# One transformer kernel, the windowed-attention stage: dense products of the gated layer, value projections and key norms assigned to other slots

## The reference, cut to what matters

```python
def _layer(x, wqkv, qs, ksc, wo, lg, lb, w1, b1, w2, b2):
    h = shift_token(x)                      # half of the features come from the token before
    q, k, v = split(h @ wqkv)               # 8 heads of 64
    q = l2norm(q) * qs; k = l2norm(k) * ksc
    q, k = rotary_xpos(q, k)
    o = local_attention(q, k, v)            # windows of 64 keys, each query sees its window and the one before
    x = x + o @ wo
    h = layernorm(shift_token(x)) * lg + lb
    a, g = split(h @ w1 + b1)               # 2 x 341, padded to 2 x 384 in the kernel
    h = a * gelu(g)
    return x + h @ w2 + b2
```

## Time and profile before

| | |
|---|---|
| median of three runs | 4851.66 us |
| the profiled execution, and its span | 4860.0 us, 4858.2 us |
| PE busy / DVE / ACT / POOL over the span | 88% / 61% / 51% / 23% |
| mean granted clock of TensorE | 0.89 |
| pass 0, first to last maximum (777.54 to 1308.02 us) | 530.48 us, granted clock 0.81 |
| pass 1, first to last maximum (1838.14 to 2348.88 us) | 510.74 us, granted clock 0.86 |

### The profile page before, as it was taken

The page is one execution under the profiler, slowest core; times in us unless marked ns, Lnnn a source line. Parts: engine busy times, 40 slices in busy tenths (PEclk is TensorE's granted clock), DMA queues, the critical chain, the costliest instruction groups (busy, mean ns, idle before and its releaser), DMA issues.

```text
span 4858.2 us, 64573 instructions
## 1 busy us (share of the span) xinstructions
PE 4266.8 (88%) x24264; PEld 2057.4 (42%) x24264; DVE 2964.9 (61%) x6559; ACT 2473.9 (51%) x4237; POOL 1116.2 (23%) x1582
## 2 busy tenths in 40 slices
PE   8888878999998889999886777999988999879999
PEld 5212335656532235555553234555553334333343
DVE  4888456656478866666345994666666653466632
ACT  3588634445348774545345553454443663236642
POOL 1100113333210013333112662111121004420024
PEclk8799977788779997988797998999996999979999
DMA  1100102111010011111000000000001000000000
GB/s 49 27 15 13 45 0 70 32 32 37 8 52 21 14 44 38 34 32 30 5 7 5 0 0 16 8 16 8 16 32 26 22 8 0 29 21 21 15 1 9
DMA packets 48024, 104.19 MB, mean 21 GB/s; under 512 B 15064, under 2 KB 15064, under 8 KB 46432
## 3 DMA queue, kind: packets, MB, share of 16 engines
q1 hardware_dynamic: 47712, 100.06, 7.6%
HBM read 40.24 MB, written 1.05 MB: 8 GB/s over the span
## 4 chain that ended last, share of the span: by engine, by line
PE 57%; DVE 17%; ACT 7%; POOL 2%; issue 2%; SPq 1%; DMA 0%; POOLq 0%; DVEq 0%; ACTq 0%
PE PS L446 29%; PE PS L1034 6%; PE PS L981 5%; DVE SM L1108 4%; DVE AR L2355 3%; PE PS L2553 2%; PE PS L1013 2%; ACT AR L453 2%; DVE AR L450 2%; PE PS L1672 1%; PE PS L1717 1%; PE PS L1662 1%; PE PS L473 1%; ACT PS L2298 1%; PE PS L986 1%
## 5 line engine op out<-in xcount | busy, mean ns | idle before, releaser
L1108 DVE TENSOR_REDUCE SM<-PS 128x1 f32<-128x512 f32 (+3 forms) x1792 | 1029.0, 627 | 256.4 <-PE PS L981 161.0
L446 PE MATMUL PS<-AR,WS 128*128 128x512 f32 (+1 forms) x2112 | 1065.8, 644 | 71.9 <-DVE AR L450 32.7
L1082 ACT ACTIVATE AR<-PS 128x1024 f32<-128x1024 f32 (+3 forms) x896 | 825.5, 933 | 338.5 <-PE PS L1016 169.2
L453 ACT ACTIVATE AR<-PS 128x512 f32<-128x512 f32 (+6 forms) x760 | 450.2, 599 | 550.2 <-PE PS L446 415.0
L981 PE MATMUL PS<-AR 51*128 51x512 bf16 (+3 forms) x1792 | 526.7, 390 | 160.9 <-DVE SM L1108 98.9
L446 PEld LDWEIGHTS PS<-AR,WS 128*128 128x128 f32 (+1 forms) x2112 | 404.0, 203 | 529.8 <-issue 406.2
L1740 ACT ACTIVATE AR<-PS,SM 128x128 f32<-128x128 f32 x512 | 229.6, 452 | 472.8 <-DVE SM L1803 470.6
L1034 PE MATMUL PS<-AR 128*32 128x512 f32 (+3 forms) x3584 | 448.6, 573 | 1.3 <-ACT AR L1082 0.9
L981 PEld LDWEIGHTS PS<-AR 51*128 51x128 bf16 x1792 | 129.9, 94 | 678.5 <-DVE SM L1108 477.0
L1013 PE MATMUL PS<-AR 51*128 51x512 bf16 (+3 forms) x1792 | 386.3, 366 | 11.8 <-ACT AR L1082 11.0
L1141 POOL CAST MBT<-SM 128x8 bf16<-128x8 f32 x128 | 28.0, 219 | 1274.3 <-DVE SM L1112 1053.9
(11 more groups left out here) (314 smaller groups left out, 7285.2 us busy)
## 6 DMA issues: line engine op xcount, KB each, us to landing
TP<-RAW SPq DMA_DIRECT2D x512, 64.0 KB, 2.0
AR<-AR SPq DMA_DIRECT2D x768, 32.0 KB
WS<-wall SPq DMA_DIRECT2D x4, 3654.5 KB, 11.1
WS<-wall SPq DMA_DIRECT2D x8, 902.5 KB, 4.6
WS<-wall SPq DMA_DIRECT2D x2, 3334.5 KB, 10.9
WS<-wall SPq DMA_DIRECT2D x1, 2384.0 KB, 9.1
WS<-wall SPq DMA_DIRECT2D x1, 1543.5 KB, 6.2
AR<-pad SPq DMA_DIRECT2D x88, 12.0 KB
```

Source lines behind the costliest of these rows:

```text
L446: t = e.matmul(o, l, r, start=(n == 0), stop=(n == len(pairs) - 1))
L453: return e.activation(o, i, ACT.Copy, scale=1.0)
L1082: e.activation(pv[:, :, off:512], sv[:, :, off:512], ACT.Exp, scale=scale).then_inc(*F.at_exp.up((s, u, p2)))
L1108: e.tensor_reduce(mh[:, at, k0 // 512:k0 // 512 + 1], bank(ring(n + g), m), AX.X, ALU.max, negate=True).then_inc(*F.at_max.up((s, k, i, rr ...
```

## The change

The products of the gated layer of chunk q leave slot 16 q + 39 (n = 7) for three slots, one `gate` and one `up` in each of n = 7, 8 and 11, for q = 0 to 5; `down` goes from n = 8 to n = 13. Norm 3 goes from n = 4 to n = 5, with it the steps of its root from n = 5, 6, 7 to n = 6, 7, 8; v1 goes from n = 11 to n = 12 (in groups with g > 0). What runs behind the units (q = 6, 7) keeps its slots. The number of arithmetic instructions stays; the number of DMAs too.

```diff
-        def gate_slot(q):
-            return 16 * q + 39 if q < 6 else (133, 138)[q - 6]
+        def gate_slots(q):
+            return [16 * q + n for n in (39, 40, 43)] if q < 6 else [(133, 138)[q - 6]] * 3
 
         def down_slot(q):
-            return gate_slot(q) + (2 if q == 6 else 1)
+            return 16 * q + 45 if q < 6 else (135, 139)[q - 6]
...
-                second = [("norm", g, j) for j, at in enumerate((2, 3, 4, 4, 6, 7, 10, 11)) if n == at] + second
+                second = [("norm", g, j) for j, at in enumerate((2, 3, 4, 5, 6, 7, 10, 11)) if n == at] + second
...
-                second += [("v", g, j) for j, at in enumerate((8, 11, 14, 15) if g else (8, 11, 12, 12)) if n == at]
+                second += [("v", g, j) for j, at in enumerate((8, 12, 14, 15) if g else (8, 11, 12, 12)) if n == at]
...
-                if slot_ == gate_slot(q):
+                if q >= 6 and slot_ == gate_slots(q)[0]:
                     first += [("gate", q, 0), ("up", q, 0), ("gate", q, 1)]
                     second += [("up", q, 1), ("gate", q, 2), ("up", q, 2)]
+                if q < 6 and slot_ in gate_slots(q):
+                    first += [("gate", q, gate_slots(q).index(slot_))]
+                    second += [("up", q, gate_slots(q).index(slot_))]
...
-                if g < 8 and n in (5, 6, 7):
+                if g < 8 and n in (6, 7, 8):
                     next(roots[g, 1], None)
```

## The result

The changed kernel takes 4914.48 us (median of four runs, 4905.77 to 4921.73), the one before 4849.32 beside it on the same chip (four runs, 4843.34 to 4854.41): ratio 1.0131, 95% interval 1.0116 to 1.0147. The forecast of 4869 had the direction; the time lies 45 us above it and outside the range of 4828 to 4900. The profiled execution took 4919.5 us, 59.5 more than that of before (4860.0); the forecast for it was +17.

The account below looks back on a forecast made before the run. TensorE, busy 88%, was read as the main bound, VectorE binding some slots. Seven groups at +2.9 and three at -1.7 (+15), group 7 +10, groups 0 and 1 -8: +17, 4877 profiled, median 4869, range 4828 to 4900.

Parts of the forecast that it names:

- 66.9: Groups 2 to 6: us for a group without a fall at n = 10, against a mean of 68.6 before.
- The Gelu alone between two exps: n = 7 and 8: table load, Gelu and product delay VectorE's next maximum; slots of 5.5 and 5.9 us.
- The fall behind n = 4: TensorE's clock drop after n = 4's two norms goes, as at most one norm stands between two products.
- I take seven of ten: Groups 2 to 6, both passes: seven of ten groups have a clock fall at n = 10; bounds none and all.
- +4.6 a fall: Cost in us of a clock fall at n = 10, summed over n = 10 to 13.
- In 0 and 1, n = 11 loses a product on TensorE, and the fall behind n = 4 goes: -2 each: Groups 0 and 1, both passes: 2 us saved in each of four groups, -8; bounds 0 and -16.
- v1 fits beside it: 0: n = 12: VectorE's 3.85 us stays and v1 adds nothing.
- group 7 at +5 each: Group 7, both passes: clock falls more easily with nothing dense in n = 9 and 10; +10 together, bounds -1 and +6 each.
- B: Rival: the clock holds from n = 4 to n = 12, no +4.6 in any group; -27, 4825 us; chance 0.27.
- C: Rival: clock falls in every group, `down` at half clock to its end; +40 or more, 4892 to 4900; chance 0.14.
- `down` wakes the clock: n = 14 and 15: they take 4.2 and 2.9 us against 5.38 and 4.20, -2.5; if the clock stays low, 0.
- D: Rival: Gelu waits hidden, 0.5 us less in each of n = 7, 8 and 11; -18 against forecast, 4851; chance 0.17.

Follow-up runs that it names:

- the held versions of before that have it moved: Kernel before with norm 3 moved and unread idle products in TensorE's list at n = 12 and 13, ratio 0.9896; with more idle products elsewhere, 0.9904.
- norm 3 and the split: Kernel before with norm 3 moved, gate and up in three slots and `down` at n = 13, v1 left in n = 11: 4886.31 us, ratio 1.0068.

## Why the prediction failed, and what of it held

**Right: the direction, the waits, and the prices at full clock.** A group put together from the measured slots without a fall before n = 13 is about 67.0 (with n = 13 at 8.3); the forecast had 66.9. The sum hides two small errors that cancel, n = 4 at 5.91 in the mean (6.15) and n = 5 and 6 at 7.31 (6.98). The Gelu alone between two exps does hold VectorE until 5.45 (5.5) and 5.85 (5.9), `down` behind the wait for its bank makes n = 13 6.6 (6.4), 8.4 in the mean with the fall (8.4). The fall behind n = 4 is gone in all ten groups, as forecast. Removing the Gelus removed the falls from n = 7 to 12 as well, and did nothing that the ratio can tell in the kernel before.

**Wrong: "I take seven of ten".** It was ten of ten. The bound was in the text; I took a value inside it because pass 1 fell less than pass 0 in the earlier trace rows. Five of the ten stand at a place that I priced at full clock, n = 7. A fall behind n = 6, where TensorE has a product, a wait of 0.09 us and norm 4, turns up only in kernels with norm 3 moved and nothing added in n = 6: one group of ten with norm 3 alone, three and four in the held versions of before that have it moved, two with norm 3 and the split, five in the changed kernel. But the changed kernel without its Gelus has the same n = 5 and 6, the wait too, and none. So what stands in n = 5 and 6 does not settle it alone. With the six products of the gated layer behind it, it costs 1.35 us (9.64 against 8.29), since they bring the clock back in the slot; with two it costs 1.8 to 2.2 in n = 7 and in three groups 1.1 to 1.4 more in n = 8. With three idle products in n = 6 there is none in twenty groups, of two kernels. Why v1's move makes five of two, and no Gelu none, stays open; ten groups of one execution are few.

**Wrong: +4.6 a fall**, and near the mean by luck. 72.05 less 67.0 is 5.1 a group. But the five groups that fall at n = 10 and 11, the place that the 4.6 was worked out for, are 73.4 in the mean, 6.4 more; the five that fall at n = 7 are 70.7, 3.7 more. At the forecast place n = 11 takes 7.8 to 8.6, not 7.7. Further on, n = 14 is 5.04 in the mean, not 4.2, since in six groups a part of it is still at 1.2 GHz, and n = 12 is 5.6 to 5.9 in four groups, where I had 5.1 in seven. Ten at 5.1 against seven at 4.6 are 19 us, the whole miss of groups 2 to 6.

**Wrong: "In 0 and 1, n = 11 loses a product on TensorE, and the fall behind n = 4 goes: -2 each".** +4.3 each: 25 us of the miss, the largest single one. The step reasoned from the earlier trace rows, a group at full clock, and took "v1 fits beside it: 0" along. Of the +17.4 in four groups, n = 11 to 13 are 10.4, n = 7 to 10 7.7 and n = 4 to 6 1.8; n = 14 and 15 give 2.5 back. Two things are behind it. Norm 3 moved into a stretch of low clock: in groups 0 PEclk is 0.50 from n = 0 to 4, and norm 3 alone costs them 3 us each. One window of pass 0's group 0 and one of its group 1 would have warned of that:

```profile
777.54:842.81 65.27, 63.24 (x461) 39.65 (x462) 36.50 (x108) 28.45 (x88) 20.59 (x25) 0.66 0.14 33
842.81:907.81 65.00, 63.51 (x534) 41.35 (x536) 39.87 (x121) 29.01 (x90) 21.52 (x26) 0.76 0.15 34
```

And v1 did not move into such a stretch, its move brings one: before, n = 12 stood at 0.81 to 0.95 in these groups, and with v1 gone from n = 11 it is at 0.50 to 0.57, with v1 alone moved and in the change. There a product does not fit beside VectorE's 3.85 (5.0 to 6.0). In groups 2 to 6 of the change gate 2 and up 2 take v1's place in n = 11; groups 0 and 1 have none. No row of before shows this; it had to be run. The 7.7 of n = 7 to 10, more than half of it in pass 1's group 1, where the clock stays low from n = 7 on, are not traced further.

**Wrong: group 7 at +5 each.** It was -0.7 and +2.3: n = 7 and 8 came as forecast (4.9 and 4.4), and in pass 1 n = 7 saves 3.3 and n = 12 to 14 0.5, while n = 9 to 11 cost 2.3 more and n = 0 to 3, at a low clock, 3.8. This and 6 us outside the groups, not costed, nearly cancel: 19 + 25 - 8 + 6 = 42, which is the distance from +17 to +59.5 within rounding.

**The rivals.** B (the clock holds) is what the added idle products made by force: 4848 there, not 4825, since they and groups 0 and 1 cost. C came closest, in the fall in every group and in that n = 14 gains next to nothing (5.04 against 5.13 in the mean). Its reason holds in seven groups of ten: the last of the six instructions of `down` takes 0.82 to 1.06 us there, 0.59 in the other three, where the clock came back before it. So "`down` wakes the clock", on which the forecast of n = 14 rested, came late in the seven, in n = 14. C's 4900 is still 14 short, for it shared the -8 of groups 0 and 1. D is refuted by n = 7 and 8.

**Drain and idle time.** The Trainium skill, ScalarE: Activation LUTs, section What ACT_TABLE_LOAD costs, would add a drain of some 1380 ns to each load. By an estimate from the Trainium skill's figure 48 such drains are 66 us, and the miss is 42, so it tempts. The trace does not agree. A Gelu starts 1.29 us after its load starts here (2169.89 to 2171.18 on ScalarE in n = 8), and the load itself 0.02 us after the exp before it has ended (2169.87), and n = 7 and 8 are 5.45 and 5.85, 0.05 under the sum without a drain. The Trainium skill, TensorE: Matmul & The Clock Gate, section HAM oscillation, ties the fall to idle time. This trace does not agree at n = 7: the fall there came behind slots of 3.49 busy in 3.49 and 3.73 in 3.82.

## What to carry to other kernels

Price a moved operation at the clock of the place where it lands, and ask what the place that it leaves does without it: v1 in n = 12 was free at 2.4 GHz (3.84 in the changed kernel without Gelu) and cost 2 us at 1.2 (5.9), and it was its own leaving of n = 11 that brought the low clock there. Look in each stretch between two dense blocks at what TensorE does and not at its busy time alone. In this kernel it paid to keep the functions of one table together in one slot. Where a kernel already loses to the clock, a few unread products at TensorE's waits are worth a try; here they gave 37 us, more than the 27 at which rival B priced this reordering.

## What the runs showed that I had not expected

- Idle products pay: 0.96 us of them in n = 12 and n = 13 each bring PEclk from 0.50 to 1.00 up to n = 15, pass 1's group 3 from 67.6 to 63.0, the kernel to 0.9923.
- TensorE at 100% busy does not keep its clock: of 7.35 us in n = 7 all are busy, at PEclk 0.56, behind a slot of one product, a norm (2 columns) and the transposes and scores.
- A fall moves rather than goes: with n = 11 thinner it comes in n = 12 instead of 13; with `down` taken from n = 8, n = 11 rises from 3.84 to 5.09 in the mean; with eight idle products in n = 10, four groups of ten still fall, with twelve there and ten more in n = 9 and 11 none does, and what fills n = 12 is paid where the clock has fallen (6.4 to 6.7 against 5.6 to 5.9).
- A wait can come from a shared bank and not from the operand: with norm 3 one slot later, norm 4 stands 0.09 us in n = 6 for VectorE's reading of norm 3, though its own square had been ready for 2.4 us.
